# Attention scores over 64 rows: key-major banks of one head beside query-major halves of the other

## The chip, the cores and the metric

One NeuronCore of a Trainium2 chip runs the whole program. The metric is the device time of one execution in microseconds (us); lower is better.

## The reference

The input is x, 8 batches of 512 tokens of 128 numbers. Two stages follow each other, each with a residual and a layer norm:

```python
x = layernorm(x + attention(x))   # 16 heads of 8 numbers, causal, softmax, output projection
x = layernorm(x + moe(x))         # 14 experts, 2 of them per token, 128 -> 256 -> 128, gelu
```

In attention each head has scores Q K^T / sqrt(128), a causal mask, a softmax over the keys and a product with V.

## The kernel before, in words

A batch has four **groups** (`c` = 0 to 3) of four heads, so attention has 32 groups. A head is stored as `(e, h)` in a group: `h` says which half of the 128 rows its split numbers stand on (rows 0 to 63 or 64 to 127), `e` is the other index of the tile. Each head has only 8 numbers, but they are split into bf16 parts, and with the row maxima they fill 64 rows.

Every group's scores are made twice.

- **Query-major** (`score_unit`, L973 and L981): queries on the partitions. These serve only to find each row's maximum. A group has five *units* `u`, each two PSUM banks of 512 columns, one for each `h`. The stationary operand is `qst` over all 128 rows, the moving one is `kst[:, c, h]`, of which one half of the rows is zero, so that only head `h` counts. A last matmul (L981, `bident` and `bmask`) adds the causal mask to the diagonal blocks. The VectorE reduces a unit to maxima (L1338) and increments `s_reduced`. There are two slots of `ps_s`, so a unit waits until the unit two before it has been reduced.
- **Key-major** (`score_bank`, L996): keys on the partitions, ten banks of 512 columns in a group, in two slots of `ps_t`. The maxima are already inside `qst` (two more rows in each half). The ScalarE takes the exponential of a bank (L808) into `probs`, the GpSimd zeroes what lies above the diagonal (L686, six selects in a group), and `pv` (L1014, fp32, four column tiles of 32) multiplies with V.

The order of the TensorE is written out by hand. In the body of group `c` it loops over ten steps `k`: key-major bank `k` of this group; at `k` = 1, 3, 5, 7, 9 the unit 0, 1, 2, 3, 4 of the group two ahead; the turn of the maxima (L1026) at `k` = 3, before unit 1; `pv` of the group before at `k` = 6 (512 columns wide), 7 (384) and 9 (the two narrow tiles); and in fixed places the projections (`PE` L1033, L1040, L1064), the output projection (L1072) and the ranks (L1082). The engines each walk through their own instructions in order, and semaphores hold them together. On the VectorE the order around a group is: unit 4 of one group, the split of the maxima, the transpose and normalisation of a `pv` result, then units 0, 1, 2, 3, 4, with the statistics and the top-2 search of an earlier batch between them.

The turned maxima go from ScalarE's queue by two small DMAs into `qst` (L848). They are issued at `k` = 6, and bank 0 of the next group waits for them.

The waits of the old unit and of the old bank:

```python
if not (isinstance(n, int) and n < 2):
    pe.wait_ge(S["s_reduced"], n - 1)      # score_unit: at k = 1, 3, 5, 7, 9, after bank k
...
if not (isinstance(n, int) and n < 2):
    pe.wait_ge(S["exp_done"], n - 1)       # score_bank
```

The functions that the diff touches, and what calls them:

## Time and profile before

| | |
|---|---|
| time, median of 3 runs | 556.04 us (553.85 to 556.76) |
| profiled execution, span from first to last instruction | 521.5 us |
| median less that span | 34.5 us |
| TensorE matmul busy | 445.9 us, 86% |
| VectorE busy | 398.1 us, 76% |
| ScalarE busy | 332.2 us, 64% |
| GpSimd busy | 282.0 us, 54% |
| mean granted TensorE clock | 0.968 |

The profile gives the profiled execution by its span alone; a time around it is not given apart from the span. Attention fills about the first 360 us; after it the experts run over sorted tiles of tokens. PE is the matmul side of the TensorE, PEld its weight loads, DVE is the VectorE, ACT the ScalarE, POOL the GpSimd. A matmul's duration in the profile is its columns' time and a tail of about 0.16 us in which the next one already runs, so distances between starts are read, not durations. The records of some matmuls are missing: of L996 the profile has 480 of 512.

### The profile page before, as it was taken

The page shows a single profiled execution, that of the slowest core. Times are in us where ns is not written, and L with a number is a line of the kernel's source. Part 1 is how long each engine was busy: PE and PEld are TensorE (multiplying, and loading weights), DVE is VectorE, ACT ScalarE, POOL GpSimd, SP SyncE. Part 2 cuts the span into 40 slices and gives each one's busy share as a digit, 9 for nine tenths or more (in the row PEclk, how much of TensorE's full clock was granted, in tenths as well). Part 3 has the DMA queues.
Part 4 walks back from the last instruction along what each step waited for, and adds up shares of the span by engine and source line. Part 5 has one row for each costly group of instructions (what it writes and reads, how often), then busy time and mean ns, then how long its engine had stood idle before and what let it go on. Part 6 is the DMA issues. An engine that isn't in the chain of part 4 may idle for free.

```text
span 521.5 us, 12373 instructions
## 1 busy us (share of the span) xinstructions
PE 445.9 (86%) x3556; PEld 267.2 (51%) x3589; DVE 398.1 (76%) x974; ACT 332.2 (64%) x809; POOL 282.0 (54%) x455
## 2 busy tenths in 40 slices
PE   6788999999999978999999999986869988884880
PEld 2354444445445433544544544532759877774870
DVE  5987779989988966998899899886787756660192
ACT  4285666865875763687587576584578978881045
POOL 6022234235834732573584475587577777777263
PEclk9999999999999997999999999998979999999796
DMA  5656386533443342343344333113144333331564
GB/s 162 197 156 180 105 286 192 161 117 118 139 142 109 107 155 85 111 130 126 108 124 157 105 91 100 38 49 95 53 120 136 104 104 92 90 90 36 163 208 116
DMA packets 74394, 64.56 MB, mean 124 GB/s; under 512 B 9030, under 2 KB 68685, under 8 KB 74336
## 3 DMA queue, kind: packets, MB, share of 16 engines
q1 hardware_dynamic: 68528, 55.08, 36.3%
q0 software_dynamic: 4512, 8.54, 4.9%
q8 instruction: 25, 0.41, 0.3%
q10 hardware_dynamic: 1296, 0.27, 0.3%
q14 instruction: 33, 0.27, 0.2%
HBM read 36.88 MB, written 25.46 MB: 120 GB/s over the span
## 4 chain that ended last, share of the span: by engine, by line
PE 47%; DVE 13%; issue 10%; DMA 9%; ACT 7%; POOL 6%; SPq 4%; another core or an unknown queue 1%; ACTq 1%; DVEq 0%; POOLq 0%
PE psum L1014 12%; PE psum L996 9%; PE psum L973 9%; DVE nmax L1338 7%; DMA o_dram<-probs,xs 4%; PE psum L981 4%; POOL o_dram L762 3%; PE psum L1033 3%; DMA experts<-o_dram 3%; DMA xs<-xs_dram 2%; PE psum L1040 2%; PE psum L1072 2%; ACT probs L808 2%; PE psum L1199 2%; PE psum L1180 2%
## 5 line engine op out<-in xcount | busy, mean ns | idle before, releaser
L808 ACT ACTIVATE probs<-psum 128x512 f32<-128x512 f32 x320 | 181.9, 595 | 107.4 <-PE psum L996 76.8
L1338 DVE TENSOR_REDUCE nmax<-psum 128x2 f32<-128x1024 f32 (+3 forms) x224 | 197.7, 912 | 32.8 <-PE psum L981 31.3
L686 POOL TENSOR_SCALAR_AFFINE_SELECT probs<-probs 128x256 f32<-128x256 f32 (+1 forms) x192 | 88.8, 488 | 140.2 <-ACT probs L808 139.6
L973 PE MATMUL psum<-kst,qst 128*128 128x512 bf16 (+2 forms) x511 | 111.0, 303 | 6.5 <-DVE nmax L1338 5.9
L996 PE MATMUL psum<-qst,kst 128*128 128x128 bf16 (+3 forms) x480 | 102.0, 297 | 6.8 <-ACT probs L808 3.1
L1014 PE MATMUL psum<-probs,vst 128*32 128x512 f32 (+3 forms) x1024 | 91.0, 452 | 1.7 <-POOL probs L686 1.5
L762 POOL DMA_INDIRECT o_dram<-probs,xs x77 | 78.0, 1013 | 26.0 <-issue 16.9
L981 PE MATMUL psum<-bmask,bident 128*128 128x256 bf16 (+1 forms) x320 | 81.0, 253 | 0.1
L996 PEld LDWEIGHTS psum<-qst,kst 128*128 128x128 bf16 x512 | 39.6, 98 | 71.4 <-ACT probs L808 34.0
L973 PEld LDWEIGHTS psum<-kst,qst 128*128 128x128 bf16 x512 | 47.9, 98 | 33.3 <-DVE nmax L1338 10.2
L917 ACT ACTIVATE hT_sb<-psum,w_cur 128x128 f32<-128x128 f32 x154 | 48.1, 364 | 7.9 <-PE psum L1180 7.2
L1199 PE MATMUL psum<-w_cur,hT_sb 128*128 128x128 f32 x308 | 48.6, 281 | 3.9 <-DVE probs L1550 3.0
L1557 DVE COPY w_cur<-experts 128x642 f32 x77 | 41.4, 541 | 12.4 <-DVE probs L1550 4.2
L1180 PE MATMUL psum<-xsT,w_cur 128*128 128x128 f32 x308 | 48.5, 281 | 0.0
L1199 PEld LDWEIGHTS psum<-w_cur,hT_sb 128*128 128x128 f32 x308 | 41.4, 196 | 5.2 <-ACT hT_sb L917 2.9
L1180 PEld LDWEIGHTS psum<-xsT,w_cur 128*128 128x128 f32 x308 | 41.6, 196 | 0.2 <-ACT xsT L908 0.2
L1550 DVE TENSOR_TENSOR probs<-psum,w_cur 128x128 f32<-128x128 f32 x77 | 22.2, 289 | 23.2 <-PE psum L1199 21.3
L981 PEld LDWEIGHTS psum<-bmask,bident 128*128 128x128 bf16 x320 | 31.5, 98 | 12.5 <-issue 0.9
L1014 PEld LDWEIGHTS psum<-probs,vst 128*32 128x32 f32 x1024 | 22.5, 110 | 24.8 <-issue 19.5
L908 ACT ACTIVATE xsT<-psum 128x128 f32<-128x128 f32 x77 | 21.2, 275 | 19.4 <-PE psum L1170 19.0
L1170 PE MATMUL psum<-ident,xs 128*128 128x128 f32 x77 | 23.5, 305 | 11.3 <-DMA xs<-xs_dram 10.8
L943 ACT ACTIVATE xr<-xr,fin_off,fin_rs 128x128 f32<-128x128 f32 x32 | 12.6, 480 | 31.9 <-POOL fin_off L790 31.9
(199 smaller groups left out, 558.8 us busy)
## 6 DMA issues: line engine op xcount, KB each, us to landing
kst<-dk SPq DMA_DIRECT2D x62, 128.0 KB, 2.8
qst<-dq SPq DMA_DIRECT2D x31, 256.0 KB, 3.1
xs<-xs_dram SPq DMA_DIRECT2D x77, 66.0 KB, 1.9
experts<-o_dram SPq DMA_DIRECT2D x7, 512.0 KB, 4.6
dk<-k SPq DMA_DIRECT2D x7, 384.0 KB, 3.0
dq<-q SPq DMA_DIRECT2D x7, 384.0 KB, 3.0
xT_sb<-in_xT SPq DMA_DIRECT2D x8, 256.0 KB, 2.8
xTv_sb<-in_xT SPq DMA_DIRECT2D x8, 256.0 KB, 2.7
```

The costliest lines, as they stand in the source:

```text
L686: pool.affine_select(out=view, in_=view, compare_op=ALU.is_ge, fill=0.0, base=0, pattern=[[0, view.shape[1]], [1, P]], channel_multiplier= ...
L762: pool.indirect_dma_start(o_dram, bass.IndirectOffsetOnAxis(xs[:, u, D:D + 1].bitcast(I32), 0), y_sb[:, u, :], None, bounds_check=TOPK * N ...
L808: act.activation(probs[:, c % 2, p, kk * T:(kk + 1) * T], ps_t[:, k % 2, :], ACT.Exp, scale=SCALE).then_inc(S["exp_done"], 1)
L917: last = act.activation(hT_sb[:, u % 2, P * ch:P * ch + P], psum[:, 2 + u % 2, P * ch:P * ch + P], ACT.Gelu, bias=w_cur[:, u % WR, B1_AT + ...
L973: pe.matmul(bank[:, at:at + w], qst[:, c, e, P * i:P * i + P], kst[:, c, h, e, 0:w], start=(at == 0), stop=False, skip_group_check=True)
L981: pe.matmul(diag_blocks, bident[:], bmask[:, 0:diag_blocks.shape[1], :], start=False, stop=True, skip_group_check=True).then_inc(S["s_fill ...
L996: last = pe.matmul(ps_t[:, k % 2, at % T:at % T + w], kst[:, c, g % 2, pair, P * j:P * j + P], qst[:, c, pair, P * j:T], start=True, stop= ...
L1014: last = pe.matmul(ps_o[32 * g:32 * g + 32, P * j:T], vst[:, j, 4 * c + g, :], probs[:, c % 2, g // 2, at:at + w], start=(j == 0), stop=(j ...
L1180: last = pe.matmul(psum[:, 2 + u % 2, P * ch:P * ch + P], w_cur[:, u % WR, P * ch:P * ch + P], xsT[:, u % 2, :], start=True, stop=True)
L1199: last = pe.matmul(y_bank(j), hT_sb[:, u % 2, P * ch:P * ch + P], w_cur[:, u % WR, W2_AT + P * ch:W2_AT + P * ch + D], start=(ch == 0), st ...
L1338: last = dve.tensor_reduce(o, i, AX.X, ALU.max, negate=True)
L1557: dve.tensor_copy(w_cur[:, j % WR, :], experts[:].rearrange("p e f -> p (e f)")[:, bass.ds(found[j // LOOK][j % LOOK], WCOLS)]).then_inc(S ...
```

## The change

All score products now contract over 64 rows. `kst` loses its zero halves, and one DMA loads it where there were two. Step `k` makes key-major bank `k` of one head on rows `64*(k%2)` and up, and beside it half of unit `k//2` for the other `h`, on the other 64 rows. The key-major banks are put in another order (`KEY_PARTS`), so that a bank has one head where its tile is wide. A unit's masks are four matmuls over 64 rows instead of two over 128. The wait for the unit's slot stands ahead of the even step's first matmul. The GpSimd has five selects in a group instead of six.

```diff
-        kst = sb("kst", [P, NG, 2, 2, T], BF16)
+        kst = sb("kst", [P, NG, 2, T], BF16)
...
-        probs = sb("probs", [P, 2, 2, 5 * T])
+        probs = sb("probs", [P, 2, NBANK * T])
...
-        PV_MASKS = {0: 4, 1: 4, 3: 5, 2: 6}
+        PV_MASKS = {0: 3, 1: 3, 3: 4, 2: 5}
+        NMASK = 5
+
+
+        KEY_PARTS = ([((e, 0, 0),) if tiles == 0 else ((e, 1, 0), (e, 3, 3 * P))
+                      for e in range(2) for tiles in range(2) for _ in range(2)]
+                     + [((0, 2, 0), (1, 2, 2 * P))] * 2)
...
-                for h in range(2):
-                    sp.dma_start(kst[64 * h:64 * h + 64, c, h, :, :],
-                                 dk[odd].rearrange("(c e h) d r t -> c h (d r) e t", h=2, e=2)[c, h]
-                                 ).then_inc(qk_loaded[c], 16)
+                sp.dma_start(kst[:, c, :, :], dk[odd].rearrange("(c e h) d r t -> c (h d r) e t", h=2, e=2)[c]
+                             ).then_inc(qk_loaded[c], 16)
...
+            pool.memset(bmask[:, :, 0:HALF], 0.0).then_inc(S["masks_ready"], 1)
+            pool.memset(bmask[:, :, HALF:P], NEG).then_inc(S["masks_ready"], 1)
+            pool.memset(place[:], 0.0).then_inc(S["masks_ready"], 1)
...
+            def scores(b, c, k, sb_, sc_):
+
+                u, half = k // 2, k % 2
+                by_key, by_query = live(b), live(sb_)
+                if by_key:
+                    bank_free(b, c, k)
+                if by_query and half == 0:
+                    unit_free(sb_, sc_, u)
+                mine, other = slice(HALF * half, HALF * half + HALF), slice(HALF - HALF * half, P - HALF * half)
+                unit = ps_s[:, (sc_ + u) % 2, 1 - half, :]
+                for n in range(2):
+                    if by_key and n < len(KEY_PARTS[k]):
+                        e, j, at = KEY_PARTS[k][n]
+                        last = pe.matmul(ps_t[:, half, at:at + T - P * j], kst[mine, c, e, P * j:P * j + P],
+                                         qst[mine, c, e, P * j:T], start=True, stop=True)
+                    if by_query and n < len(UNIT_PARTS[u]):
+                        e, i, at = UNIT_PARTS[u][n]
+                        w = P * (i + 1)
+                        pe.matmul(unit[:, at:at + w], qst[other, sc_, e, P * i:P * i + P], kst[other, sc_, e, 0:w],
+                                  start=(at == 0), stop=False, skip_group_check=True)
+                if by_key:
+                    last.then_inc(S["st_filled"], 1)
+
+            def unit_masks(b, c, u):
+
+                first, step, count = ((3 * P, P, 1), (3 * P, P, 1), (2 * P, P, 2), (2 * P, P, 2), (P, 2 * P, 2))[u]
+                for rows in range(2):
+                    for h in range(2):
+                        mine = slice(HALF * h, HALF * h + HALF)
+                        blocks = ps_s[:, (c + u) % 2, h, :].rearrange("p (n w) -> p n w", w=P)[
+                            :, first // P:first // P + (count - 1) * step // P + 1:step // P, HALF * rows:P]
+                        last = pe.matmul(blocks, place[mine, HALF - HALF * rows:3 * HALF - HALF * rows],
+                                         bmask[mine, 0:count, 0:P - HALF * rows],
+                                         start=False, stop=(rows == 1), skip_group_check=True)
+                last.then_inc(S["s_filled"], 1)
...
                     for k in range(NBANK):
-                        if live(b):
-                            score_bank(b, c, k)
+                        if live(b) or live(sb_):
+                            scores(b, c, k, sb_, sc_)
+                        if k in UNIT_AT and live(sb_):
+                            unit_masks(sb_, sc_, UNIT_AT[k])
                         if k == M_AT and live(ahead(b, c, 1)[0]):
                             turn_maxima(*ahead(b, c, 1))
-                        if k in UNIT_AT and live(sb_):
-                            score_unit(sb_, sc_, UNIT_AT[k])
...
-            for h in range(2):
-                dve.memset(kst[64 * h:64 * h + 64, :, 1 - h, :, :], 0.0).then_inc(S["st_zeroed"], 1)
```

## Rows read from the trace of the kernel before

**Rows 1.** The page: engine totals, and groups of instructions by line (busy, mean ns, idle before)
```profile
PE 445.9 (86%) x3556; PEld 267.2 (51%) x3589; DVE 398.1 (76%) x974; ACT 332.2 (64%) x809; POOL 282.0 (54%) x455
...
L1338 DVE TENSOR_REDUCE nmax<-psum 128x2 f32<-128x1024 f32 (+3 forms) x224 | 197.7, 912 | 32.8 <-PE psum L981 31.3
...
L981 PE MATMUL psum<-bmask,bident 128*128 128x256 bf16 (+1 forms) x320 | 81.0, 253 | 0.1
```

**Rows 2.** Busy by stretch, groups 0 to 3: PE, PEld, DVE, ACT, POOL, clock, DMA
```profile
109.45:120.29 10.84, 10.26 (x87) 5.39 (x86) 9.44 (x19) 7.38 (x16) 4.01 (x7) 1.00 0.47 142
120.29:130.51 10.22, 9.94 (x84) 5.08 (x84) 9.18 (x24) 6.28 (x14) 6.54 (x11) 1.00 0.27 86
130.51:140.46 9.95, 9.32 (x79) 4.41 (x78) 9.59 (x22) 7.79 (x17) 7.90 (x13) 1.00 0.33 98
140.46:150.97 10.51, 10.20 (x91) 4.89 (x90) 9.39 (x23) 7.50 (x14) 4.26 (x10) 1.00 0.60 186
```

**Rows 3.** The VectorE's waits: of one batch (107.9 to 148.71), then of 60 to 340
```profile
DVE nmax L1338 <- PE psum L981: 2.6, 4, 0.8
...
DVE nmax L1338 <- PE psum L981: 24.3, 35, 2.7
```

**Rows 4.** Instructions in order of time, a group 0: start, us, engine, line
```profile
150.63 1.22 DVE L1338 TENSOR_REDUCE nmax<-psum 128x2 f32<-128x1024 f32 x1
...
152.46 1.21 DVE L1338 TENSOR_REDUCE nmax<-psum 128x2 f32<-128x1024 f32 x1
...
153.41 0.38 PE L996 MATMUL psum<-qst,kst 128*128 128x512 bf16 x1
...
153.71 1.06 PE L1014 MATMUL psum<-probs,vst 128*32 128x512 f32 x8
...
153.83 1.27 DVE L1338 TENSOR_REDUCE nmax<-psum 128x2 f32<-128x768 f32 x2
...
154.71 0.39 PE L1040 MATMUL psum<-q,nident 128*128 128x512 bf16 x1
...
154.94 0.38 PE L996 MATMUL psum<-qst,kst 128*128 128x384 bf16 x2
...
155.70 0.27 PE L981 MATMUL psum<-bmask,bident 128*128 128x256 bf16 x1
...
156.01 1.29 DVE L1338 TENSOR_REDUCE nmax<-psum 128x2 f32<-128x768 f32 x2 [0.83 <-PE psum L981]
...
156.69 0.61 PE L996 MATMUL psum<-qst,kst 128*128 128x384 bf16 x4
...
157.99 1.23 DVE L1338 TENSOR_REDUCE nmax<-psum 128x4 f32<-128x1024 f32 x1 [0.69 <-PE psum L981]
```

**Rows 5.** In order of time: units 3 of groups 1 and 2, unit 4 of group 3
```profile
125.96 1.29 DVE L1338 TENSOR_REDUCE nmax<-psum 128x2 f32<-128x768 f32 x2 [0.80 <-PE psum L981]
...
135.48 1.28 DVE L1338 TENSOR_REDUCE nmax<-psum 128x2 f32<-128x768 f32 x2
...
147.48 1.23 DVE L1338 TENSOR_REDUCE nmax<-psum 128x4 f32<-128x1024 f32 x1 [0.69 <-PE psum L981]
```

**Rows 6.** In order of time: three small matmuls of 14 columns, each with its weights
```profile
148.20 0.22 PE L1082 MATMUL psum<-hotb,ones 128*128 128x14 bf16 x3
```

**Rows 7.** In order of time, start of the kernel: a mask built, the first unit
```profile
9.70 0.29 POOL L634 TENSOR_SCALAR_AFFINE_SELECT tri<-tri 128x128 bf16<-128x128 bf16 x1
...
13.87 0.38 PE L973 MATMUL psum<-kst,qst 128*128 128x512 bf16 x1 [0.49 <-DVE qst L1303]
```

**Rows 8.** In order of time: the first maxima by DMA, and the first key-major bank
```profile
21.52 1.69 ACTq L848 DMA_DIRECT2D qst<-nmpart  x2
...
25.55 0.59 PE L996 MATMUL psum<-qst,kst 128*128 128x512 bf16 x2
```

**Rows 9.** Busy by stretch, the first 20 us and two us after a stall
```profile
0.00:20.00 20.00, 13.03 (x51) 5.41 (x53) 14.61 (x26) 6.95 (x11) 8.72 (x36) 1.00 0.65 182
...
198.00:200.00 2.00, 1.39 (x7) 0.80 (x7) 2.00 (x4) 0.31 (x1) 1.04 (x1) 0.50 0.38 125
```

More of the change, by code:

```diff
@@ L44, in post_ln_attention_moe @@
     WR = 4
+    HALF = 64
     B1_AT, W2_AT, B2_AT, WCOLS = F, F + FC, 2 * F + FC, 2 * F + FC + D
@@ L490, in store_parts @@
                         if not (isinstance(taken, int) and taken == 0):
-                            hold(qk_loaded[cc], taken * 48)
+                            hold(qk_loaded[cc], taken * 32)
                 for n in (1, 2, 3):
@@ L966, in score_unit, with bank_free @@
                     pe.wait_ge(S["s_reduced"], n - 1)
[L969 to L984 removed]
+            def bank_free(b, c, k):
                 n = (b * NG + c) * NBANK + k
@@ L990, in score_bank @@
                     pe.wait_ge(S["exp_done"], n - 1)
-                pair, kk = k // 5, k % 5
-                for g in (2 * pair, 2 * pair + 1):
-                    for j in range(NQ):
-                        at, w = seg(g, j)
-                        if at // T == kk:
-                            last = pe.matmul(ps_t[:, k % 2, at % T:at % T + w],
-                                             kst[:, c, g % 2, pair, P * j:P * j + P],
-                                             qst[:, c, pair, P * j:T], start=True, stop=True)
@@ L999, in score_bank @@
-                last.then_inc(S["st_filled"], 1)
+            def scores(b, c, k, sb_, sc_):
[19 more added lines that the diff above has]
+                    last.then_inc(S["st_filled"], 1)
@@ L1001, in pv @@
             def pv(b, c, tiles):
                 n = b * NG + c
-                pe.wait_ge(S["masked"], 6 * n + max(PV_MASKS[j] for j in tiles))
+                pe.wait_ge(S["masked"], NMASK * n + max(PV_MASKS[j] for j in tiles))
                 if 0 in tiles:
@@ L1283, in _ @@
             dve.memset(mean_w[:], 1.0 / D).then_inc(S["const_ready"], 1)
-            for h in range(2):
-                dve.memset(kst[64 * h:64 * h + 64, :, 1 - h, :, :], 0.0).then_inc(S["st_zeroed"], 1)
             dve.memset(ones[:], 1.0).then_inc(S["const_ready"], 1)
@@ L1299, in _ @@
             dve.wait_ge(S["picked"], 1)
-            dve.tensor_scalar(kst[64:P, 0, 1, 0, :], psum[64:P, 5, :], k_ones[64:P, 0:1], None, ALU.add
+            dve.tensor_scalar(kst[64:P, 0, 0, :], psum[64:P, 5, :], k_ones[64:P, 0:1], None, ALU.add
                               ).then_inc(S["stacked_dve"], 1)
@@ L1304, in _ @@
             dve.wait_ge(S["picked"], 2)
-            dve.tensor_scalar(kst[64:P, 0, 1, 1, :], psum[64:P, 6, :], k_ones[64:P, 0:1], None, ALU.add
+            dve.tensor_scalar(kst[64:P, 0, 1, :], psum[64:P, 6, :], k_ones[64:P, 0:1], None, ALU.add
                               ).then_inc(S["stacked_dve"], 1)
```

77 lines of the change are left out of this document (38 added, 39 removed).

## The prediction

> **What bounds the kernel now.** I read the page first, then the busy time by stretch, the waits, and last one group instruction by instruction. The page says TensorE: 86% busy, with the VectorE at 76% [rows 1]. Within attention the two stand closer. In the four groups of one batch (41.5 us) the TensorE is busy 9.3 to 10.3 us of each group and the VectorE 9.2 to 9.6; the ScalarE needs at most 7.8 and the GpSimd, whose records are rough, at most 7.9 [rows 2]. So the TensorE bounds most groups, with the VectorE just behind it. The waits give the size of the gap: the VectorE waits for filled units 2.6 us in a batch, four times, and 24.3 us between 60 and 340 us [rows 3]. No change to the TensorE alone can be worth more than these waits while attention stays as it is.
>
> **What the TensorE is spared.** Durations hold a tail, so I take starts. A bank of 512 columns passes in 0.22 us, the distance from 154.71 to 154.94; one mask of 256 columns takes half of that. A group has 5120 key-major columns, 5120 query-major ones and 2048 of masks. If two row halves run together, the second 5120 disappear: 2.1 us a group. The masks become 20 matmuls instead of 10, with 1536 columns in each half: 0.64 us instead of 0.85. Small matmuls with weights of their own follow each other 25 ns apart (three cost 0.22 us, of which 0.17 is one alone) [rows 6], so the ten more weight loads are no bound. That is about 2.3 us a group, 70 us over 31 groups, and nearly all of it is TensorE time that will not be time of the kernel.
>
> Against it stand the changes of the array's mode. Going from full columns to the four column tiles of the V product costs 0.09 us (153.41 plus 0.21 to 153.71) and leaving it about as much [rows 4]. No row shows a switch between 128 and 64 rows; below it is nothing, above it I allow 0.3 us, and I take the nearest row, 0.1. Eleven products of a batch (projections, their subtractions, the ranks) are of 128 rows between steps of 64: at most 22 new switches, 2.2 us a batch, most of them beside the VectorE's work.
>
> What no trace row shows is that two *row* halves run together. Column tiles do: eight instructions of the V product, each of 512 columns, pass in 0.89 us (153.71 to 154.71 less a switch), where eight times 0.22 would be 1.76 even if an fp32 column cost no more than a bf16 one [rows 4]. The bounds for a pair are 0.22 us (together) and 0.44 (one after the other). I take 0.22, the nearer kind. The Trainium skill, "TensorE: Matmul & The Clock Gate", section on packing small matmuls, gives 3.07 times for four row tiles, less than four; by that the pair would cost nearer 0.28 and the sum below would lose some 0.1 us per window. No run here shows it yet.
>
> **What decides: the slot of a unit.** Before, a unit took its slot only when all its matmuls were issued at once, after bank `k`. Now it takes it at the even step and holds it to the odd one, and what lies between is inside. For unit 3 (steps 6 and 7) that is the whole V product of tile 0. The first matmul of step 6 waits until unit 1 has been reduced, and the key-major bank, the exponential and the V product queue behind that wait.
>
> Group 0 [rows 4], counted from the end of the reduction of unit 4 before it, 147.48 + 1.23 = 148.71 [rows 5]. The VectorE ends unit 1 at 152.46 + 1.21 = 153.67, that is 4.96, without having waited, and it is free again at 6.47 (unit 2 and a cast). Unit 3 then costs from 4.96: release 0.05, step 6 0.22, switch 0.1, V product 0.89, switch 0.1, the subtraction for q 0.22, switch 0.1, step 7 0.22, masks 0.16, and 0.2 from the last column to the VectorE's start (155.70 + 0.11 to 156.01). Sum 2.26, filled at 7.22. The VectorE waits 0.75 (before: 0.83). It ends unit 3 at 8.50. The TensorE meanwhile does V's second product (0.88 with both switches, 155.81 to 156.69), steps 8 and 9 (0.44), masks 0.16 and latency 0.2: filled 1.48 after the last column at 7.02, at 8.70. Wait 0.2 (before 0.69). The unit ends at 9.93 instead of 159.22 - 148.71 = 10.51. **Group 0 gains 0.58 us.**
>
> Group 1 waited 0.80 ahead of unit 3 [rows 5]. There the product with Wo waits for the VectorE's sum over y, which lies after unit 1, so step 6 starts 0.9 later than the slot is free; but between units 2 and 3 the VectorE has 1.0 us of its own. The wait shrinks to about 0.4: gain 0.4. Group 2 did not wait: unit 3 came at 135.48, right behind unit 2 and a part of the top-2 search, and the VectorE was busy 9.59 of 9.95 [rows 2, 5]. With step 6 released at 4.22 unit 3 is filled at 6.1, and the VectorE is free for it at 6.3: gain 0. Group 3 waited 0.69 ahead of unit 4 [rows 5] and a trifle ahead of unit 3; by group 0's sum it will wait 0.3 and 0.2: gain 0.3. A batch gains 1.3 us of 41.5.
>
> Six batches are of this kind: 8 us. For the first and last batch, and the stretch at half clock after the stall near 195 us, where columns cost double [rows 9], I add 2 us by estimate. The experts' part starts that much earlier and keeps its length. Sum 10 us: 521.5 - 10 = 511.5 for the profiled span, and with the 34.5 that the median has over it, **546 us**.
>
> **Edits at no cost.** The GpSimd's longer masks (seven more instructions of about 0.3 us): it has built the last old one at 10.0, and the first unit starts at 13.87 [rows 7]; without that cover up to 2 us once. The dropped memsets end long before as well. One DMA for `kst` instead of two frees SyncE's queue of 31 issues; nobody is seen waiting for it. Five selects instead of six have the same elements within a tenth, and the one for tile 2 is larger and last, but its V product is nine steps away. The maxima's DMA must land before bank 0: its two issues ended at 23.21 and the bank ran at 25.55, so it lands within 2.34 us [rows 8]; by the sum above it gets at least 3. The turn of the maxima now stands behind unit 1's masks, and so no longer holds that unit back. The ScalarE has 10 banks as before, 7.8 of 9.9 us in its worst group; waits for the VectorE come to it later by half a microsecond and it has that much to give.
>
> **Rivals.** (1) *The halves do not overlap.* Then every step costs 0.22 more and each pair of masks 0.16; unit 3's window in group 0 grows by 0.6 and unit 4's too, so that group ends at 11.1, 0.6 later than before. Groups 1, 2 and 3 lose 0.2, 0.75 and 0.85 likewise: 2.4 a batch, 16 us with the ends: 572. For it: no row shows 64-row tiles. Against: column tiles do overlap. It decides from about 0.33 us a pair on. Chance 0.12.
> (2) *The switches or the slot eat the gain.* With 0.2 to 0.3 us a switch, the six in units 3's and 4's windows of group 0 cost 0.5 and more, and nothing is left: 556. The Trainium skill, "TensorEngine Tiling", key properties, says that changing the tiling mode drains the engine; that agrees with the 0.09 us here, and leaves the row kind open. Chance 0.16.
> (3) *The VectorE never waits.* If fills come early because its other work covers the windows better than I reckon, all 24.3 us of waits go: 532. For it: in group 2 it is so already. Against: unit 3's window, 2.26, is longer than unit 2's 1.27. Chance 0.12.
> (4) *The clock falls.* A less busy TensorE could be set to 1.2 GHz; after the stall it was granted half [rows 9]. Then the engine's 7.8 us a group become about 14, and 31 groups cost 115 us more: 670. Against: 65% busy in the first 20 us at full clock [rows 9]; the new share is 75 to 80%. Chance 0.02. By the Trainium skill, "TensorE: Matmul & The Clock Gate", section on the clock gate, an idle stretch brings the slow state; the stall's rows agree.
> The forecast itself has 0.58.
>
> **Numbers.** Faster or slower by 0.5% (2.8 us) is about what can be told from no change. Faster: 0.58 and 0.12, of which a little falls within the bound: 0.69. Same: 0.16. Slower: 0.12, 0.02 and the far end of the switches: 0.15. The range reaches from 533, close to rival 3, to 560, past rival 2 with its dear switches; the serial and the clock case are left out.
>
> **What will show it.** Pairs: starts of the two halves less than 0.05 us apart, steps 0.22 apart. TensorE's time in a group's stretch at about 8 us. Batches of 40.2 us. The VectorE's waits halved, and those left ahead of unit 3, in groups 0, 1 and 3, with the TensorE waiting for the VectorE at steps 4 and 6 as it does not now. Steps of 0.4 us would prove the forecast wrong, and so would a wait ahead of unit 3 above 1 us, or bank 0 held by the maxima's DMA.

## The result, and the profile after

| | before | after |
|---|---|---|
| time, median | 556.4 us (553.85 to 557.14) | 562.01 us (558.5 to 564.37) |
| ratio | | 1.011 [1.0074, 1.0146] |
| profiled execution, span | 521.5 us | 560.9 us |
| mean granted TensorE clock | 0.968 | 0.887 |

The kernel is 1.1% slower where 546 us and "faster" had been forecast. The two spans must not be compared. On some chips the same program's experts' part is some 30 us shorter than on others, and the shown profile of before comes from such a chip, its times from the other kind; c_before below shows the kernel before on the kind of the times. Every ratio here is taken on one chip.

The page of after: engine totals, TensorE's clock in 40 slices, and groups by line.

```profile
PE 426.6 (76%) x3895; PEld 242.4 (43%) x3909; DVE 389.1 (69%) x972; ACT 333.0 (59%) x809; POOL 278.0 (50%) x429
...
PEclk9659899999998979899799879879768998989996
...
L1367 DVE TENSOR_REDUCE nmax<-psum 128x2 f32<-128x1024 f32 (+3 forms) x224 | 198.2, 914 | 46.5 <-PE psum L1028 45.3
...
L1010 PE MATMUL psum<-qst,kst 64*128 64x384 bf16 (+3 forms) x512 | 119.5, 323 | 49.7 <-DVE nmax L1367 23.2
```

The TensorE's busy time fell although its clock fell too, but the VectorE waits for it more than before, 45.3 us against 31.3 [rows 1]. Between 60 and 340 us these waits should have halved from 24.3 us [rows 3]; they are 34.6 us. And the TensorE now waits for the VectorE: 23.2 us ahead of L1010, the key-major product, behind the wait for a unit's slot.

Busy by stretch for the same four groups as in [rows 2] (turn of the maxima to turn; PE, PEld, DVE, ACT, POOL, clock, DMA):

```profile
115.13:125.20 10.07, 8.34 (x99) 4.05 (x96) 8.74 (x19) 7.47 (x16) 5.47 (x8) 1.00 0.47 159
125.20:134.74 9.54, 7.96 (x98) 3.95 (x94) 8.78 (x24) 6.44 (x15) 4.51 (x9) 1.00 0.35 108
134.74:146.39 11.65, 9.10 (x87) 3.28 (x87) 9.58 (x22) 7.58 (x16) 8.18 (x13) 0.85 0.24 66
146.39:157.20 10.81, 8.43 (x103) 3.56 (x100) 9.77 (x23) 7.63 (x14) 4.17 (x9) 1.00 0.54 180
```

Groups 0 and 1 gained 0.77 and 0.68 us, more than forecast. Group 2 lost 1.70: its clock is 0.85, the one below 1. Group 3 lost 0.30. Together 42.07 us where before had 41.52.

Group 2 in order of time (start, us, engine, line):

```profile
136.54 0.39 PE L1010 MATMUL psum<-qst,kst 64*128 64x512 bf16 x1 [1.59 <-DVE nmax L1367]
136.54 0.55 PE L1015 MATMUL psum<-kst,qst 64*128 64x384 bf16 x3
136.77 0.38 PE L1010 MATMUL psum<-qst,kst 64*128 64x512 bf16 x1
...
137.82 0.50 PE L1010 MATMUL psum<-qst,kst 64*128 64x384 bf16 x1 [0.51 <-DVE nmax L1367]
...
138.36 1.93 PE L1046 MATMUL psum<-probs,vst 128*32 128x512 f32 x8
...
140.62 0.46 PE L1028 MATMUL psum<-bmask,place 64*128 64x256 bf16 x4
```

```profile
139.59 0.21 DVE L1474 TENSOR_REDUCE top<-tm 128x4 f32<-128x56 f32 x1
141.59 1.29 DVE L1367 TENSOR_REDUCE nmax<-psum 128x2 f32<-128x768 f32 x2 [1.79 <-PE psum L1028]
```

The pair works as forecast: L1010 and L1015 start at the same hundredth (136.54) and the next step follows 0.23 us later. But step 4 has waited 1.59 us for the VectorE and step 6 another 0.51; behind these waits the V product of tile 0 takes 1.93 us instead of 1.06 [rows 4], and the VectorE waits 1.79 us for unit 3, where before it did not wait at all [rows 5]. The prediction had named a wait above 1 us ahead of unit 3 as a sign that it is wrong; this is one.

The stretches of the whole of attention (by the same columns; first after, then c_before):

```profile
12.00:68.00 56.00, 44.96 (x372) 19.43 (x373) 41.45 (x65) 29.22 (x59) 9.06 (x20) 0.76 0.48 146
68.00:304.00 236.00, 190.77 (x2071) 84.13 (x2081) 200.88 (x453) 160.49 (x327) 112.19 (x186) 0.94 0.44 139
304.00:344.00 40.00, 30.86 (x329) 12.61 (x321) 32.10 (x75) 21.90 (x46) 19.99 (x33) 0.83 0.23 71
```

```profile
12.00:68.00 56.00, 48.65 (x362) 24.87 (x368) 45.47 (x73) 32.66 (x66) 11.00 (x24) 1.00 0.55 164
68.00:304.00 236.00, 220.72 (x1820) 109.49 (x1842) 203.63 (x457) 158.18 (x324) 115.23 (x210) 0.99 0.44 135
304.00:344.00 40.00, 36.89 (x318) 18.21 (x323) 36.06 (x85) 24.87 (x53) 24.54 (x43) 1.00 0.23 71
```

In all three the clock is lower after. The start and the last batches (0.76 and 0.83 against 1.00) are hit most.

### The profile page after: what moved, and what is told of

The parts are those of the page before. It is cut to its first block, busy times and chain, and to the rows that moved or that the text cites. A ratio compares the mean times of both kernels' runs of the same rounds, so it can differ in the third digit from the quotient of the medians.

```text
span 560.9 us, 13004 instructions
## 1 busy us (share of the span) xinstructions
PE 426.6 (76%) x3895; PEld 242.4 (43%) x3909; DVE 389.1 (69%) x972; ACT 333.0 (59%) x809; POOL 278.0 (50%) x429
## 4 chain that ended last, share of the span: by engine, by line
PE 46%; DVE 26%; issue 11%; ACT 5%; another core or an unknown queue 4%; DMA 4%; POOL 1%; SPq 1%; ACTq 1%; DVEq 0%; POOLq 0%
DVE nmax L1367 13%; PE psum L1046 12%; PE psum L1010 8%; PE psum L1230 6%; PE psum L1211 6%; DVE ov L1375 3%; PE psum L1028 3%; PE psum L1201 3%; PE psum L1065 3%; DMA experts<-o_dram 2%; PE psum L1015 2%; ACT probs L829 1%; PE psum L1072 1%; DVE rz L1377 1%
## 5 line engine op out<-in xcount | busy, mean ns | idle before, releaser
L1367 DVE TENSOR_REDUCE nmax<-psum 128x2 f32<-128x1024 f32 (+3 forms) x224 | 198.2, 914 | 46.5 <-PE psum L1028 45.3
L708 POOL TENSOR_SCALAR_AFFINE_SELECT probs<-probs 128x512 f32<-128x512 f32 (+1 forms) x160 | 84.5, 549 | 153.6 <-ACT probs L829 151.5
L1010 PE MATMUL psum<-qst,kst 64*128 64x384 bf16 (+3 forms) x512 | 119.5, 323 | 49.7 <-DVE nmax L1367 23.2
L1015 PE MATMUL psum<-kst,qst 64*128 64x384 bf16 (+3 forms) x512 | 117.0, 325 | 3.7 <-DVE nmax L1367 2.5
L1046 PE MATMUL psum<-probs,vst 128*32 128x512 f32 (+3 forms) x1024 | 102.8, 500 | 0.0
L1010 PEld LDWEIGHTS psum<-qst,kst 64*128 64x128 bf16 x512 | 35.3, 96 | 134.9 <-ACT probs L829 60.1
L1211 PE MATMUL psum<-xsT,w_cur 128*128 128x128 f32 x308 | 55.4, 308 | 16.3 <-ACT xsT L929 15.4
L1028 PE MATMUL psum<-bmask,place 64*128 64x128 bf16 (+2 forms) x640 | 52.6, 243 | 0.0
L1028 PEld LDWEIGHTS psum<-bmask,place 64*128 64x128 bf16 x640 | 36.1, 102 | 16.1 <-issue 4.5
L1015 PEld LDWEIGHTS psum<-kst,qst 64*128 64x128 bf16 x512 | 34.9, 97 | 8.5 <-issue 3.7
L1375 DVE STREAM_TRANSPOSE ov<-psum 128x512 f32<-128x512 f32 x32 | 22.8, 712 | 6.0 <-issue 4.1
```

The source lines that it names most:

```text
L708: pool.affine_select(out=view, in_=view, compare_op=ALU.is_ge, fill=0.0, base=0, pattern=[[0, view.shape[1]], [1, P]], channel_multiplier= ...
L1010: last = pe.matmul(ps_t[:, half, at:at + T - P * j], kst[mine, c, e, P * j:P * j + P], qst[mine, c, e, P * j:T], start=True, stop=True)
L1015: pe.matmul(unit[:, at:at + w], qst[other, sc_, e, P * i:P * i + P], kst[other, sc_, e, 0:w], start=(at == 0), stop=False, skip_group_chec ...
L1028: last = pe.matmul(blocks, place[mine, HALF - HALF * rows:3 * HALF - HALF * rows], bmask[mine, 0:count, 0:P - HALF * rows], start=False, s ...
L1046: last = pe.matmul(ps_o[32 * g:32 * g + 32, P * j:T], vst[:, j, 4 * c + g, :], probs[:, c % 2, at:at + w], start=(j == 0), stop=(j == 2), ...
L1211: last = pe.matmul(psum[:, 2 + u % 2, P * ch:P * ch + P], w_cur[:, u % WR, P * ch:P * ch + P], xsT[:, u % 2, :], start=True, stop=True)
```

## The experiments

All are read in one way. T1 is the start of the turn of the maxima in group 0's body of batch 1, T3 that in group 2's body of batch 7, the last in attention, T2 that in group 2's body of batch 6; between stand 22 stretches (T1 to T2) and four (T2 to T3). The last columns are the stretches of batch 2, differences of starts. The expectations name a stretch by the groups whose maxima are turned, one ahead: their "from group 3's to group 0's turn", "into group 0", is group 2's stretch in [rows 2] and here. Kernels that share a letter in the column "chip" were timed on one chip. The recorded clock of a stretch is given where it matters. The kernel after itself was not timed on chips B and D, so there its nearest runs stand beside the others (e_late on B, e_start on D).

| kernel | chip | ratio to before [95%] | T1 | T2 | T3 | g0 | g1 | g2 | g3 |
|---|---|---|---|---|---|---|---|---|---|
| c_before | A | 1.001 [0.9994, 1.0025] | 67.81 | 304.31 | 344.67 | 10.84 | 10.22 | 10.13 | 10.52 |
| c_after | A | 1.017 [1.0139, 1.02] | 69.55 | 306.94 | 352.78 | 9.96 | 9.54 | 11.53 | 10.58 |
| e_twice | A | 1.0585 [1.0565, 1.0605] | 75.15 | 328.20 | 375.31 | 10.89 | 10.24 | 11.87 | 11.44 |
| e_pv5 | A | 0.9931 [0.9906, 0.9957] | 67.75 | 296.90 | 338.88 | 9.90 | 9.15 | 11.60 | 9.71 |
| e_before5 | B | 1.004 [1.0024, 1.0057] | 68.08 | 304.34 | 344.11 | 10.84 | 10.09 | 10.07 | 10.51 |
| e_late | B | 1.0094 [1.0061, 1.0127] | 67.91 | 301.55 | 346.16 | 9.97 | 9.53 | 11.11 | 10.56 |
| e_warm | B | 1.0137 [1.0102, 1.0171] | 75.38 | 305.13 | 349.48 | 10.04 | 9.53 | 10.39 | 10.79 |
| e_warm5 | B | 0.9833 [0.9794, 0.9871] | 74.87 | 296.11 | 334.86 | 9.91 | 9.14 | 10.29 | 9.79 |
| c_after2 | C | 1.0152 [1.011, 1.0194] | 72.35 | 306.36 | 350.11 | 10.06 | 9.53 | 11.60 | 10.79 |
| e_warm_in | C | 1.0126 [1.0081, 1.017] | 72.74 | 306.39 | 350.33 | 9.96 | 9.54 | 11.13 | 10.79 |
| e_pv5_again | C | 0.994 [0.9912, 0.9969] | 72.12 | 299.02 | 342.06 | 9.90 | 9.15 | 11.18 | 9.84 |
| e_best | C | 0.9833 [0.9774, 0.9893] | 65.48 | 289.35 | 332.91 | 9.91 | 9.14 | 11.14 | 9.71 |
| e_start | D | 1.0106 [1.0075, 1.0136] | 67.88 | 303.79 | 349.76 | 9.95 | 9.54 | 11.48 | 10.63 |
| e_start5 | D | 0.9901 [0.987, 0.9932] | 68.50 | 294.55 | 336.66 | 9.90 | 9.15 | 11.59 | 9.70 |
| e_wide | D | 1.0129 [1.0088, 1.017] | 68.20 | 303.41 | 348.44 | 9.96 | 9.54 | 11.63 | 10.55 |
| e_wide5 | D | 0.984 [0.9809, 0.9871] | 67.69 | 291.62 | 331.80 | 9.91 | 9.14 | 11.17 | 9.71 |
| e_scatter | C | 1.0149 [1.009, 1.0209] | 71.42 | 307.94 | 354.99 | 10.06 | 9.53 | 11.70 | 10.93 |
| e_scatter5 | C | 0.9823 [0.9785, 0.9862] | 67.58 | 292.58 | 333.82 | 9.90 | 9.15 | 10.39 | 10.16 |

**c_before and c_after: both kernels unchanged, side by side.**

> The kernel before, unchanged, as a control of the comparison and for a second profile. All theories: ratio 1.00 within 0.005. Its profiled span was 521.5 us with a clock of 0.968 while the median run took 556; theory CHANCE (the profile shown was an unusually quick execution, in which the clock fell seldom) expects a span nearer 550 and a mean clock nearer 0.9 here; theory OVERHEAD (34 us lie outside every span) expects 521 again.

> The changed kernel again. Theory CLOCK (pairs do overlap and save time, but a less busy TensorE is set to half clock once a batch in group 2 or 3, and each such spell costs 1.5 to 2 us) expects the same spells near the end of group 2 in nearly every batch, a mean clock of 0.87 to 0.91 and a ratio of 1.005 to 1.015. Theory SLOT (the gain goes into the longer hold of the unit's slot alone) expects batches of about 41.5 us also where the clock is full. Theory CHANCE expects the spells in other places and other numbers.

The kernel before has a span of 557.3 us and a time of 559.43 in its profiled execution here, so only 2.1 us lie outside the span, and the "34.5 us outside the span" of the prediction do not exist: attention ends as in the shown profile (T3 344.67 against 343.55), and what follows takes 212.6 us instead of 178.0. The kernel after loses 8.1 us by T3, as much as the medians differ (563.85 - 555.64 = 8.2), though the two profiled executions differ by 3.7 us only, since c_before's takes 4.4 us more behind T3. The 8.1 us are 1.7 up to T1, 0.9 in the 22 middle stretches, 5.5 in the last four. The shown profile of after (T1 73.68, T2 308.15, T3 353.79) and c_after2, each beside c_before, lose 5.9 and 4.5 up to T1, gain 2.0 and 2.5 in the middle, and lose 5.3 and 3.4 in the last four: the loss lies at the ends in all three. A batch in the middle neither gains nor loses: -0.88, -0.68, +1.40, +0.06.

**e_pv5: V's first product behind step 5**, where no slot is held.

```diff
-        PV_AT = {6: (0,), 7: (1,), 9: (3, 2)}
+        PV_AT = {5: (0,), 7: (1,), 9: (3, 2)}
```

> The first V product moves from step 6, inside unit 3's hold of its slot, to step 5, behind unit 2. Theory SLOT: the wait ahead of unit 3 (0.63 us in groups 0 and 3) goes, 1.3 us a batch, some 9 us in all: ratio to before about 0.995. Theory CLOCK: the same waits go where the clock is full, but the TensorE then waits longer for the VectorE in group 2, the spells stay, and the ratio stays at 1.00 to 1.01.

2.4% less than the kernel after, and 0.7% less than before. Busy by stretch, batch 2:

```profile
107.03:116.93 9.90, 8.19 (x98) 4.04 (x95) 8.72 (x19) 7.46 (x16) 5.45 (x8) 1.00 0.50 161
116.93:126.08 9.15, 7.79 (x98) 3.98 (x94) 8.85 (x24) 6.34 (x15) 4.51 (x9) 1.00 0.39 115
126.08:137.68 11.60, 9.19 (x88) 3.36 (x88) 9.60 (x22) 7.37 (x16) 8.55 (x13) 0.85 0.25 72
137.68:147.39 9.71, 8.36 (x104) 3.56 (x101) 9.40 (x23) 7.63 (x14) 3.86 (x9) 1.00 0.59 194
```

Groups 1 and 3 gain 0.39 and 0.87 us more; from T1 to T2 it is 8.2 us, from T2 to T3 3.9, before T1 1.8. Group 2 stays at 11.60 and a clock of 0.85. The VectorE's waits ahead of unit 3 fall from 0.66 to 0.20 us in group 1 and from 0.54 to nothing in group 3; in group 0 (0.80 to 0.74) and group 2 (1.74 to 1.72) they stay.

**e_twice: each key-major product issued twice** (the second overwrites the first).

> The changed kernel with every key-major product issued twice (the second overwrites the first with the same numbers), so that the TensorE streams about 5120 more columns a group on one row half, its load of before. Theory CLOCK: with the load back, the spells at half clock in attention are rarer than in the changed kernel, mean clock of attention above 0.96; the time is the changed kernel's or less, ratio 0.99 to 1.005. Theory SLOT: every step is 0.22 us longer, each hold of the slot 0.44, the VectorE waits more, 0.5 to 1 us a group: ratio 1.03 to 1.05.

Ten products of 0.22 us in 32 groups are 70 us more TensorE time, and the kernel is 23 us slower than after. The half-clock slices of the middle are rarer (mean clock 0.96 between 68 and 304 us against 0.93), but group 2 still takes 11.87, at a clock of 1.00. Work on the critical engine everywhere is no cure, and the run does not separate a clock from a slot.

**e_before5: the same placing in the kernel before.**

> The kernel before, with the V product of tile 0 behind step 5 instead of 6 and nothing of the change. It tells whether the 12 us that this placing gave after the change (563.9 to 551.7) belong to the change. Theory SLOT (the placing pays only because a unit holds its slot over two steps): no gain here, 554 to 558, since unit 3 was issued at once behind step 7 and unit 2 at once behind step 5. The rival (the placing is good in any version): 545 to 550 here too, and then the change itself is worth nothing even with it.

1.004: no gain, even 0.4% lost. So the 2.4% belong to a unit that holds its slot over two steps, as only the change made it.

**e_late: the wait for the slot behind the key-major half.**

```diff
-                if by_query and half == 0:
-                    unit_free(sb_, sc_, u)
...
+                    if by_query and half == 0 and n == 0:
+                        unit_free(sb_, sc_, u)
```

> The kernel after, with the wait for a unit's slot moved behind the key-major half of the step, so that the ScalarE's bank no longer queues behind the VectorE. In a step that waits, the halves then run one after the other (0.22 us more ahead of that unit, three or four steps a group). Theory CLOCK: TensorE's idle stretches are the same length less 0.2 us each, the spells stay, and the time stays within 2 us of the kernel after (562). Theory SLOT: the ScalarE and so the masks and the V product come earlier, worth up to 0.3 us a group, less 0.2 for the serial halves: within 3 us either way. A gain of over 5 us would say that the bank's queueing is what costs.

1.0094, in the range of both theories; the gain of over 5 us that would have made the ScalarE's queueing the cost is not there. A smaller one is not excluded: against the 1.011 to 1.017 of the kernel after on other chips it would be up to 4 us.

**e_warm and e_warm5: fillers in group 2's body**, on after and on e_pv5.

```diff
+                if by_key:
+                    for _ in range({2: 2, 4: 5, 6: 2}.get(k, 0) if c == 2 else 0):
+                        e, j, at = KEY_PARTS[k][0]
+                        pe.matmul(ps_t[:, half, at:at + T - P * j], kst[HALF * half:HALF * half + HALF, c, e, P * j:P * j + P],
+                                  qst[HALF * half:HALF * half + HALF, c, e, P * j:T], start=True, stop=True)
                 if by_query and half == 0:
                     unit_free(sb_, sc_, u)
```

> The kernel after, with nothing taken out; in the body of group 2 alone, where TensorE stands waiting ahead of steps 2, 4 and 6 (0.54, 1.58 and 0.5 us in the profile), it issues the key-major product of the step 2, 5 and 2 times more ahead of that wait (same bank, overwritten by the real one; at 0.22 us a time, 2.0 us a batch). Theory CLOCK (the once-a-batch fall of the granted clock to half, right behind those waits, is what costs the kernel its gain): the half-clock spell near 137 to 141, 178 to 182 and 226 to 230 is gone, the V product after it takes 1.06 us instead of 1.9, the interval from group 3's to group 0's turn of the maxima falls from 11.5 to about 10.1, and the time falls by 1.3 us x 6 to 7 batches, 8 to 10 us, to 0.98 to 0.985 of the kernel after, 553 to 556 us, although TensorE does more work. Theory SLOT (the interval of 11.5 comes from unit 3's late slot and the V product in it, at whatever clock): the interval stays at 11.5 or grows, and the time stays or rises by up to 3 us.

> The fillers of the run before this one, on the version that issues the V product of tile 0 at step 5 instead of 6 (551.7 us, where the interval into group 0 is still 11.6). Theory CLOCK: that interval falls to about 10, and with it the time by 8 to 10 us more, to 542 to 544 us: the two gains add, since they lie in different groups. Theory SLOT: with the slot's window short already, nothing is left to gain: 551 to 553.

Between 62 and 196 us no slice of 2 us is under 0.8 of the clock any more, the V product takes 1.06 us, and group 2 takes 10.39 and 10.29: that much CLOCK had right. The time did not follow. On after the ratio is 1.0137: group 3 stays at 10.79, and the fillers of batch 0 stand where nothing waited (that group takes 15.15 us, 12.47 in e_warm_in), so T1 comes at 75.4. From T1 to T3 it takes 274.1 us, 4.2 less than e_late on the same chip, where 8 to 10 were expected. On e_pv5 the ratio is 0.983, one point better than the 0.993 of chip A, despite as late a T1. The size was overrated by half.

**e_warm_in: the fillers from batch 1 on; c_after2 and e_pv5_again beside it.**

> The kernel after, unchanged, beside the three that follow, on their chip (two chips gave different lengths of the experts' part, so a ratio is only good on one chip). Its ratio to the kernel before was 1.017 and 1.011: by every theory it is 1.010 to 1.018 again, with intervals from group 3's to group 0's turn of the maxima of about 11.5 us and half the clock inside them.

> The fillers in group 2's body again (2, 5 and 2 key-major products more ahead of the waits of steps 2, 4 and 6), but from the second batch on: in the first batch the profile of the run with them everywhere showed no wait there that they fill, and a stretch of 15.2 us where the kernel after took 10.9. Theory CLOCK, with the first 65 us left as they are: from the first turn of the maxima of batch 1 to the last of all it takes 274 us, as with the fillers everywhere, where the kernel after takes 280 to 283; so the ratio to the kernel after on this chip is 0.983 to 0.990, and it ends level with the kernel before (0.995 to 1.003 of it). Theory SLOT: the same time as the kernel after, within 0.4%.

> The V product of tile 0 behind step 5, nothing else changed from the kernel after, beside the kernel after on one chip. It was 0.993 of the kernel before where the kernel after was 1.017. Expected again: 0.990 to 0.996 of before; the intervals of groups 0 to 2 are 9.7 to 10.1, 9.9 and 9.15 us and the one into group 0 stays at 11.6, at half the clock.

The controls repeat (1.015 and 0.994). The fillers give nothing here: 1.0126, T1 to T2 233.7 us against 234.0, although the record shows full clock in group 2. The same stretch, in order of time, e_warm_in first and e_warm (chip B) second:

```profile
134.49 0.22 PE L1063 MATMUL psum<-bident,nmq 128*32 128x128 bf16 x1 [0.19 <-DVE ov L1380]
...
138.00 1.06 PE L1051 MATMUL psum<-probs,vst 128*32 128x512 f32 x8
139.23 0.33 PE L1033 MATMUL psum<-bmask,place 64*128 64x256 bf16 x4
...
140.63 0.96 DVE L1372 TENSOR_REDUCE nmax<-psum 128x2 f32<-128x768 f32 x1 [1.09 <-issue]
```

```profile
135.76 0.22 PE L1063 MATMUL psum<-bident,nmq 128*32 128x128 bf16 x1 [0.18 <-DVE ov L1380]
...
139.28 1.06 PE L1051 MATMUL psum<-probs,vst 128*32 128x512 f32 x8
140.51 0.33 PE L1033 MATMUL psum<-bmask,place 64*128 64x256 bf16 x4
...
140.88 0.96 DVE L1372 TENSOR_REDUCE nmax<-psum 128x2 f32<-128x768 f32 x1
```

From the turn on, TensorE's rows are the same to 0.01 us (V product at 3.51 and 3.52, masks at 4.74 and 4.75), and yet the VectorE begins unit 3 at 6.14 on one chip and at 5.12 on the other, where it had been free since 5.05. A TensorE row gives a modelled end; the VectorE's start is what shows when the unit was there. The Trainium skill, "Perfetto Trace Analysis", section on the lifecycle of a Tensor Engine instruction, says that the profiler computes this end instead of observing it; the two fences agree.

**e_best: step 5, fillers in group 2, in the last batches and in the start.** Four key-major products ahead of step 4 in three groups of batches 6 and 7, and, ahead of the units of the first two bodies:

```diff
+                if not by_key and by_query and half == 0 and u:
+                    for _ in range(3):
+                        pe.matmul(ps_t[:, 1, 0:2 * P], bident[:], bmask[:].rearrange("p n w -> p (n w)"), start=True, stop=True)
```

> The V product behind step 5 with fillers in three places: in group 2's body from the second batch on (as in the run before), four key-major products ahead of step 4's wait in the last batches' groups that have no projections and wait there 1.3 to 1.5 us, and, ahead of the units of the start, three products of the mask with the identity into an unused bank (0.33 us of columns per unit, ahead of waits of 0.5 to 0.7 us), so that the clock does not fall at 17 us as it did in the kernel after. Theory CLOCK: the first turn of batch 1 comes at 67 to 69 us instead of 75, the stretch from there to the last at 264 to 269 us, and the ratio to the kernel before is 0.965 to 0.978. Theory SLOT: 0.983 to 0.993, as without them.

T1 comes at 65.48, 6.6 us earlier than e_pv5_again's and with no slice of 2 us under 0.8 of the clock before 190 us; by T3 it leads by 9.2. The ratio is 0.983 [0.9774, 0.9893], short of CLOCK's 0.965 to 0.978 and at the edge of SLOT's. T1 alone proves little, for e_pv5 without fillers had it at 67.75 and e_pv5_again at 72.12. In the last batches the fillers gave nothing: 43.6 us from T2 to T3 against 43.0, the clock still at 0.72 in group 0 of batch 7, and 11.34 us for the group behind it at full clock.

**e_start and e_start5: the start's fillers alone**, on after and on e_pv5.

> The kernel after with fillers in the start alone: ahead of each unit of the two groups that run before the first key-major bank, three products of the mask with the identity into an unused bank (0.33 us of columns each time, ahead of waits of 0.5 to 0.7 us for the VectorE). Nothing changes behind 35 us. Theory CLOCK for the start: no slice below full clock before 50 us, the first turn of the maxima of batch 1 at 65 to 68 us (it is at 69.6 to 73.7 in the kernel after, 67.8 before), and the ratio to before falls from 1.015 to 1.002 to 1.008. Theory SLOT, for which the start plays no part: 1.010 to 1.018.

> The same fillers in the start, with the V product of tile 0 behind step 5. The two act in different stretches, so the ratios should add: 0.994 less the 0.7 to 1.2% of the run before this one, 0.982 to 0.988. If it ends there, the fillers in group 2's body, which the version with all of them (0.983) had besides, gave nothing.

Two stretches of the start, c_after and then e_start:

```profile
16.00:20.00 4.00, 3.17 (x24) 1.34 (x18) 4.00 (x6) 0.00 (x0) 0.00 (x0) 0.55 0.95 310
20.00:36.00 16.00, 12.52 (x76) 4.96 (x76) 10.57 (x16) 7.19 (x14) 0.99 (x2) 0.58 0.34 106
```

```profile
16.00:20.00 4.00, 3.46 (x34) 1.59 (x32) 4.00 (x7) 0.00 (x0) 0.00 (x0) 1.00 0.98 315
20.00:36.00 16.00, 12.09 (x115) 5.90 (x118) 13.33 (x19) 9.66 (x18) 1.99 (x4) 1.00 0.38 117
```

The fillers keep the full clock, and 115 matmuls pass in 16 us instead of 76; T1 is at 67.88 and 68.50, as before the change. In ratios the start is worth about 0.4% (1.0152 to 1.0106, 0.994 to 0.9901, across chips, intervals touching), less than the 0.7 to 1.2% expected.

**e_wide and e_wide5: fillers of group 2 over all 128 rows**, on after and with step 5 and the start's fillers. Against e_warm_in:

```diff
-                        pe.matmul(ps_t[:, half, at:at + T - P * j], kst[HALF * half:HALF * half + HALF, c, e, P * j:P * j + P],
-                                  qst[HALF * half:HALF * half + HALF, c, e, P * j:T], start=True, stop=True)
+                        pe.matmul(ps_t[:, half, at:at + T - P * j], kst[:, c, e, P * j:P * j + P],
+                                  qst[:, c, e, P * j:T], start=True, stop=True)
```

> The fillers in group 2's body from the second batch on, over all 128 rows of the array instead of 64 (same place, same number, 0.22 us each), on the kernel after. With the 64-row fillers on this kind of chip the record showed full clock, and yet the VectorE's unit 3 began 6.14 us after the turn of the maxima, where on another chip the same TensorE records went with 5.12. Theory HIDDEN CLOCK (the engine still ran that V product slower than its record says, because the fillers left half the array idle): now unit 3 starts at 5.1 to 5.3 us, the stretch is 10.3 instead of 11.1, and the ratio is 0.985 to 0.990 of the kernel after, 1.000 to 1.005 of before. The rival (something else holds unit 3 on that chip): 6.1 us and 11.1 us as with 64 rows, 1.012.

> Everything together: V product behind step 5, fillers in the start, 128-row fillers in group 2's body. Theory HIDDEN CLOCK: group 2's stretch falls from 11.1 to 10.2 us in each of the batches and the ratio to before is 0.970 to 0.978. The rival: the ratio of the run with the start's fillers and step 5 alone, within 0.3%.

Group 2 stays at 11.63 and 11.17, with a recorded clock of 1.00: HIDDEN CLOCK falls. e_wide5 against e_start5 is 0.984 against 0.990, more than the rival's 0.3%; it came between T1 and T3 (264.1 us against 268.2), half of it in the last four stretches, the rest where e_start5's clock still fell.

**e_scatter and e_scatter5: the GpSimd's indirect writes out of group 2.** In batch 1 group 2 took 10.26 us in e_wide5 and 10.35 in e_warm_in, and from batch 2 on 11.1. What begins with batch 2 in that stretch are these writes:

```diff
-        SCATTER_AT = {(0, 1): (0, 1), (1, 0): (2,), (1, 1): (3,), (2, 0): (4, 5), (2, 1): (6, 7)}
+        SCATTER_AT = {(0, 1): (0, 1), (1, 0): (2,), (1, 1): (3,), (3, 0): (4, 5), (3, 1): (6, 7)}
```

> The kernel after, with the GpSimd's four indirect writes of group 2's body (x_even_second or x_odd_second to xs_dram, 0.97 us each) issued in group 3's body instead. They fall into group 2's stretch from batch 2 on and not in batch 1, and in the runs with full clock in the record batch 1's group 2 took 10.3 us and the later ones 11.1. Theory SCATTER (these writes, on the chips with the slower experts' part, hold up what TensorE's V product and its signals need): group 2's stretch falls by 0.8 us where the clock is full and the ratio is 0.988 to 0.993 of the kernel after, 1.002 to 1.008 of before, unless group 3's stretch takes the 0.8 over. Theory CLOCK: the half-clock spells stay, and with them 11.5 us and 1.011 to 1.017.

> The same move, on the version with the V product behind step 5, the start's fillers and the 128-row fillers in group 2 (0.984 of before), where no half-clock row is left in the middle batches. Theory SCATTER: group 2's stretch falls from 11.1 to 10.2 us, as in batch 1, in five or six batches, and the ratio to 0.974 to 0.979. If group 3's stretch grows by as much, the writes cost wherever a V product meets them, and the ratio stays at 0.982 to 0.986 with the 11.1 in another group. The rival (the delay belongs to group 2's own work from batch 2 on, not to the writes): 11.1 stays in group 2.

Groups 2 and 3 by stretch, e_wide5 and then e_scatter5:

```profile
126.25:137.42 11.17, 9.25 (x93) 3.58 (x94) 10.52 (x22) 7.75 (x17) 8.16 (x13) 1.00 0.25 68
137.42:147.13 9.71, 8.36 (x103) 3.56 (x101) 9.14 (x23) 7.50 (x14) 4.14 (x9) 1.00 0.59 203
```

```profile
126.14:136.53 10.39, 9.40 (x94) 3.58 (x94) 10.11 (x22) 7.65 (x17) 5.73 (x12) 1.00 0.23 64
136.53:146.69 10.16, 8.87 (x105) 3.49 (x101) 9.79 (x23) 7.51 (x14) 6.38 (x9) 1.00 0.58 191
```

And the VectorE's unit 3 in group 2 of both, with what ran ahead of it:

```profile
131.09 0.21 DVE L1482 TENSOR_REDUCE top<-tm 128x4 f32<-128x56 f32 x1
131.69 1.29 DVE L1375 TENSOR_REDUCE nmax<-psum 128x2 f32<-128x768 f32 x2 [0.38 <-PE psum L1036]
```

```profile
130.98 0.21 DVE L1482 TENSOR_REDUCE top<-tm 128x4 f32<-128x56 f32 x1
131.11 1.28 DVE L1375 TENSOR_REDUCE nmax<-psum 128x2 f32<-128x768 f32 x2
```

The ScalarE sees the same. TensorE's step 8 starts 5.43 and 5.42 us into the stretch, but its bank reaches the ScalarE at 7.01 with the writes, and without them it is there by the second exponential of this row, with no wait (e_wide5, then e_scatter5):

```profile
133.26 0.60 ACT L829 ACTIVATE probs<-psum 128x512 f32<-128x512 f32 x1 [0.80 <-PE psum L1018]
```

```profile
131.76 1.07 ACT L829 ACTIVATE probs<-psum 128x512 f32<-128x512 f32 x2
```

So it is what the TensorE delivers that comes late, and not the VectorE alone that is held. Without the writes group 2 falls by 0.78 us and the wait ahead of unit 3 is gone. The two runs are of different chips, but e_best on e_scatter5's chip has 11.14 with the writes, and both runs have 10.25 and 10.26 in batch 1, where there are none: SCATTER holds for where the 11.1 came from. The writes that lie in groups 0 and 1 from batch 2 on cost nothing (e_wide5: 9.90 and 9.22 us in batch 1, 9.91 and 9.14 in batch 2). But group 3, which has them now, grows by 0.45, and the ratio, 0.9823, does not stand apart from e_wide5's. On after alone the move gives nothing: there the clock still falls in group 2, and it takes 11.70 us without the writes. With the writes alone it is 11.1, with neither 10.39, and with the writes and one spell of half clock 11.0 to 11.8: on these chips the fall of the clock adds 0 to 0.7 us to what the writes cost. In e_pv5_again group 2 takes 11.18 and 11.11 us at a clock of 0.85 and 11.04 twice at full clock, within one execution.

## Why the prediction was wrong

Two steps failed. Every term was priced at full clock, with rival 4, its fall, at 0.02; and unit 3 of group 2 was summed as filled at 6.1, where it came at 8.05, of which the clock is a part and not the whole. They show in two terms of the sum: group 2 (gain 0) and the ends (2 us more).

**The pairs: right.** The halves start together, steps are 0.22 to 0.23 us apart and not 0.28, the TensorE's time in a full-clock group is 8.0 to 8.4 us. Rival 1 (572) fell; so did rival 3, since the VectorE waits more, not never. Of rival 2 the switches fell: from the V product's start to the next 64-row step 1.00 us pass (138.00 to 139.00 in e_warm_in), as from 153.71 to 154.71 before [rows 4]. Its slot stayed, at another price.

**Groups 0 and 1: right, and too small.** 0.77 and 0.68 us gained where 0.58 and 0.4 were summed. In group 0 the VectorE waits 0.89 and 0.20 us, where 0.75 and 0.2 were summed.

**Group 2: here the sum failed.** "With step 6 released at 4.22 unit 3 is filled at 6.1, and the VectorE is free for it at 6.3: gain 0." Counted as there, from the end of unit 4 (132.32 + 1.22 = 133.54), the slot was released at 4.22 and the VectorE free at 6.26, as forecast, but unit 3 reached it at 141.59 - 133.54 = 8.05. Two things were left out. A TensorE that has less to do waits, in this group 1.59 and 0.51 us ahead of steps 4 and 6, and behind these waits the granted clock is half: from the V product's start to step 7's 1.86 us pass, where 0.99 were summed. And on chips C and D what the TensorE delivers in that window comes later when the indirect writes of the GpSimd lie in it (0.8 us). Either alone keeps the group above 11 us there; with both taken away it is 10.39 (e_scatter5).

**Group 3 and the slot.** A gain of 0.3 was summed; it was a loss of 0.3 in batch 2 (0.03 to 0.4 in batch 2 of the other runs of this kernel's order, up to 0.5 gained in later batches). The window of unit 3 was named as what decides, and that is right: with V's first product outside it group 3 gains 0.81 us on before, and a batch takes 40.36 us where the prediction had 40.2. The forecast let group 3's other work cover all but 0.2 us of the window; the wait ahead of unit 3 was 0.54, and with the V product outside it was gone.

**The ends: failed.** "For the first and last batch ... I add 2 us by estimate." They lost 1.7 us up to T1 (4.5 in c_after2, 5.9 in the shown profile) and 3.4 to 5.5 in the last four stretches, where no projection fills the waits and the clock is 0.83. This, with the 8 us of the middle that came as -0.9 to 2.5, is what makes the kernel slower and not merely level. T1 goes with the time spent at half clock ahead of it (twice what the mean clock from 12 us on lacks of 1): 65.5 with none (e_best), 67.6 to 67.9 with 3.4 us (e_scatter5, e_wide5, e_start), 69.6 with 17 (c_after), 72.1 and 72.4 with 24 (e_pv5_again, c_after2), 73.7 with 27 (after), by estimate 0.3 us for each. For the start e_start, whose fillers kept the clock, bears this out; for the last batches no run separates the clock from the slot.

**The clock, rival 4: named, and dismissed for a wrong reason.** It got 0.02, as a clock that falls everywhere or not at all; "65% busy in the first 20 us at full clock" was the argument. It fell in places: a mean over a stretch does not show how the pauses lie in it. The kernel before was never below full clock in attention but behind the loop's stall (198 to 204 us); the kernel after is at 0.76, 0.94 and 0.83 in the three stretches above. The Trainium skill, "TensorE: Matmul & The Clock Gate", section on HAM oscillation, tells of a kernel whose waits between bursts of matmuls bring the slow clock again and again; group 2 agrees in kind, by far shorter waits (1.59 and 0.51 us, with V at 1.93 instead of 1.06).

**The number.** The span was taken for an execution of the same kind as the times, and 34.5 us were put outside it. On the chips of the times they lie in the experts' part, so the sum was not hurt by the mistake: 10 us off 556 stays 10 us off.

**What stays open.** On chip B the fall of the clock in group 2 costs 0.7 us (11.11 in e_late, 10.39 in e_warm), and the same writes at the same places leave no delay; on chip C taking the fall away left 11.13. Why the writes delay what the TensorE delivers on some chips and not on others was not tried; the Trainium skill, "DMA: Bandwidth & Descriptors", section on SWDGE and HWDGE, says that such writes keep their descriptor rings in the on-chip memory, which no run here bears on. Beyond that, the tail after T3 varies by several us from one execution to another.

## What to carry to other kernels

When work is taken from the engine that is nearly always busy, look for the places where it will now stand and wait: the clock behind each of them is part of the price, and a mean share does not show it. When an operation comes to hold a slot over two steps instead of one, move everything long out of the two; here one number in a table turned 1.5% slower into 0.6% faster. A few useless matmuls ahead of a known wait can be worth more than they cost (0.983 of before with them), but only where the engine would have waited.

## What the runs showed of the hardware

- Matmuls on the two halves of 64 rows start within 0.01 us of each other, and a pair of 512 columns passes in 0.22 to 0.23 us, as one alone did.
- The half clock comes in spells of some 3.5 to 7 us in the middle of attention (10.5 behind the loop's stall in c_after) and of up to 24 us in the start. Fillers of 0.33 us of columns per unit, ahead of waits of 0.5 to 0.7 us, kept it away there (clock 1.00 for 0.55 to 0.58).
- Two chips with TensorE rows equal to 0.01 us gave the VectorE the same unit 1.02 us apart. A matmul row's end is no proof of when its result was there.
- Chips differ in the experts' part by some 30 us (before: 523.32 us median on chip B, 555.0 on chip A) with the same attention (T3 at 343.55 in the shown profile and at 344.67 in c_before; in e_before5, on chip B, at 344.11).
- On chips C and D, at full clock, indirect writes of the GpSimd (0.97 us of it each) cost 0.8 us in group 2, 0.45 in group 3 and nothing in groups 0 and 1; on chip B the same writes cost nothing in group 2 either (10.35 us in batch 1 without them, 10.39 in batch 2 with them).
